# The causal mask of an attention stage moves from TensorE products into VectorE's row maximum

## The chip, the core and the metric

The kernel runs on one core of a Trainium2 chip. The metric is device time in microseconds: the median of three runs of the kernel before is 2123.16 us (2119.22 to 2128.04). The engines are called as in the profile: PE is TensorE, PEld its weight loads, DVE is VectorE, ACT ScalarE, POOL GpSimd, SP SyncE. All arithmetic is fp32, or fp32 split into a high and a low part for TensorE.

## The reference

Two blocks over x of 32 batches, 256 tokens, 256 features. Each block is a small conditional network, then a feed-forward part with experts. The change touches the attention in the first block:

```python
q = (x @ wq.T).reshape(B, S, N_HEADS, HEAD_DIM)        # 16 heads of 16
k = (x @ wk.T).reshape(B, S, N_KV_HEADS, HEAD_DIM)     # 4 key heads, each for 4 query heads
...
attn = jnp.einsum('bqhd,bkhd->bhqk', q, k) * scale
causal = jnp.tril(jnp.ones((S, S), dtype=bool))
attn = jnp.where(causal, attn, jnp.float32(-jnp.inf))
attn = jax.nn.softmax(attn, axis=-1)
out = jnp.einsum('bhqk,bkhd->bqhd', attn, v).reshape(B, S, C)
```

The stages around it are: a gated network whose weights are picked per batch (before it), the products of the eight routed experts, a second network with shared experts, and sixteen experts (after it).

## The kernel before

The kernel is written engine by engine, in program order, with semaphores between the engines; no scheduler reorders it. The attention stage runs over the 32 batches as a software pipeline. One call of `body(i)` on every engine works on several batches at once: the turned scores and exponentials of batch i, the scores and row maxima of batch i + 1, the projection of q, k and v of batch i + 2, the output projection of batch i - 2, and, for pairs of batches further back, the choice of experts (the picks, in every second call). An engine's order within a call is the order of the lines in its `body`.

Scores are made twice. First, with the queries on the partitions, to find each query's maximum over the keys (`scores`, L1708, and `maxima`, L1241). Then, with the keys on the partitions and the maximum subtracted inside the product (`turned_scores`, L1733), for the exponentials (`exps`, L1135), where GpSimd sets the later keys to zero (`keep_earlier`, L1035). The causal mask of the change is the one of the first scores only: it keeps later keys out of the maximum.

The first scores of a batch come in three rounds r. Rounds 0 and 1 take the second 128 queries (q = 1) with all 256 keys, two heads of each group a round. Round 2 takes the first 128 queries (q = 0) with the first 128 keys, all four heads. Each round fills four PSUM banks of 512 columns, one for each key head g, in a ring of six banks (`slot`, L886), which the turned scores use in turn with them. The products contract over 16 rows and four of them, at different rows of the array, run side by side. The mask is then added by one more product for each bank: a bf16 identity times a bf16 mask, on the 128 columns of each head in which later keys exist (L1729 to L1731). That product closes the bank and raises `scores_done`.

VectorE reduces each bank with one `tensor_reduce` to the negated maxima of its two or four heads (L1248) and raises `max_done`, twelve times a batch. TensorE waits for it at three kinds of places. It reuses a bank only when its maxima are taken (`ring_free`, L1704): the turned scores of round 0 (L1736) wait for the tenth maximum of the batch ahead, the scores of round 0 (L1712) for all twelve, those of round 1 and the turned scores of rounds 1 and 2 for others. And `turn_max` (L1773) transposes the maxima, for q = 0 when the twelfth is there, for q = 1 when the eighth is; the transposed row is copied (`keep_shift`, L1250 on VectorE and L1157 on ScalarE) and goes by a DMA into the row of the queries that the turned scores read.

In VectorE's `body` (L1516) the maxima stand between other work: `residual`, `keep_shift`, then maxima of round 0 with `norm_low` between the second and third, division and `h_low`, maxima of round 1 with `divide` and `keep_kv` between them, `keep_logits`, maxima (2, 0) and (2, 1), `out_low` (o_lo), maxima (2, 2) and (2, 3). In TensorE's `body` (L1850) the part around round 2 is: `turn_max(i, 1)`, `scores(i, 2)`, `turn_out`, `values(i, 0)`, and in the next call `turned_scores(i, 0)`, `project_out`, `turn_max(i, 0)`, `scores(i, 0)`.

The constants are prepared in the stage before: the load of `at.mask` (L196), its bf16 form and the bf16 identity on ScalarE (L308, L310).

Of the kernel before, what the change touches and what calls it, by code (L numbers as in the profile page):

```python
# [7 lines left out]
BF16 = mybir.dt.bfloat16  # L8
SP, PE = mybir.EngineType.SP, mybir.EngineType.PE
U32 = mybir.dt.uint32  # L10
ALU = mybir.AluOpType
# [3 lines left out]
P = 128  # L15
B, S, D = 32, 256, 256
TT = S // P
KT = D // P
# [53 lines left out]
class AttentionConstants:  # L72

    LOADS = 15
    HIGHS = 5 + 4 * KT
    LOWS = 2 + 4 * KT

    def __init__(self, nc, ctx, sem):
        def sb(name, shape, dt=F32):
            return ctx.enter_context(nc.sbuf_tensor(name, shape, dt))  # L80

        self.ident = sb("at_ident", [P, P])
        self.identb = sb("at_identb", [P, P], BF16)
        self.mask = sb("at_mask", [P, P])
        self.one_rows = sb("one_rows", [P, 1])
        self.maskb = sb("maskb", [P, G, P], BF16)
        self.norm = sb("at_norm", [P, KT])
        self.norm_q = sb("at_norm_q", [P, KT])
        self.wqk_raw = sb("wqk_raw", [P, KT, QB + 1, P])
        self.wqk_hi = sb("wqk_hi", [P, KT, QB + 1, P], F32R)  # L90
        self.wqk_lo = sb("wqk_lo", [P, KT, QB + 1, P], F32R)
        self.wv_raw = sb("wv_raw", [P, KT, VW])
        self.wv = sb("wv", [P, KT, 2 * VW], F32R)
        self.wo_raw = sb("wo_raw", [P, KT, D])
        self.wo_hi = sb("wo_hi", [P, KT, D], F32R)
        self.wo_lo = sb("wo_lo", [P, KT, D], F32R)
        self.norm2 = sb("norm2", [P, KT])
        self.gate_raw = sb("gate_raw", [P, KT, EM])
        self.gate = sb("gate", [P, KT, 2 * EM], F32R)
        self.earlier_raw = sb("earlier_raw", [P, P])  # L100
        self.earlier = sb("earlier", [P, P], BF16)
        self.ones = sb("ones", [P, P], BF16)
        self.iota = sb("expert_iota", [P, EM])
        self.region = sb("region", [P, EM])
        self.rules = sb("rules", [P, RULES])
        self.tile_index = sb("tile_index", [1, 3 * TILES0])
        self.own_row = sb("own_row", [P, EM])
        self.const_in = sem("at_const_in")
        self.w_hi_done = sem("at_w_hi_done")
        self.w_lo_done = sem("at_w_lo_done")  # L110


def cond_ffn_phase(nc, sem, x_t, w_ug, w_dn, cond, c0, at, front, norm_w, w_qk, one_rows, w_v, w_o, ident_in, mask_in, route_consts):
# [3 lines left out]
    with ExitStack() as ctx:  # L117
# [135 lines left out]
        def _(act):  # L253
# [50 lines left out]
            def weights_high(n):  # L304
                if n == 0:
                    act.wait_ge(at.const_in, 16 * at.LOADS)
                    nc.scalar.activation(at.norm_q[:], at.norm[:], ACT.Copy, scale=HD ** -0.5).then_inc(at.w_hi_done, 1)
                    nc.scalar.activation(at.identb[:], at.ident[:], ACT.Copy).then_inc(at.w_hi_done, 1)  # L308
                elif n == 1:
                    nc.scalar.activation(at.maskb[:], at.mask[:].unsqueeze(1).broadcast_to([P, G, P]), ACT.Copy).then_inc(at.w_hi_done, 1)  # L310
                    nc.scalar.activation(at.earlier[:], at.earlier_raw[:], ACT.Copy).then_inc(at.w_hi_done, 1)
                elif n in (2, 4):
                    t = n // 2 - 1
                    act.wait_ge(at.w_hi_done, 1)
                    nc.scalar.activation(at.wqk_hi[:, t, 0:QB], at.wqk_raw[:, t, 0:QB], ACT.Copy, scale=at.norm_q[:, t:t + 1]).then_inc(at.w_hi_done, 1)
                    nc.scalar.activation(at.wqk_hi[:, t, QB], at.wqk_raw[:, t, QB], ACT.Copy, scale=at.norm[:, t:t + 1]).then_inc(at.w_hi_done, 1)
                elif n in (3, 5):
                    t = n // 2 - 1
                    nc.scalar.activation(at.wv[:, t, 0:VW], at.wv_raw[:, t], ACT.Copy, scale=at.norm[:, t:t + 1]).then_inc(at.w_hi_done, 1)
                    nc.scalar.activation(at.gate[:, t, 0:EM], at.gate_raw[:, t], ACT.Copy, scale=at.norm2[:, t:t + 1]).then_inc(at.w_hi_done, 1)  # L320
                elif n == 6:
                    nc.scalar.activation(at.wo_hi[:], at.wo_raw[:], ACT.Copy).then_inc(at.w_hi_done, 1)
# [50 lines left out]
        def _(dve):  # L373
# [67 lines left out]
            def weights_low(n):  # L441
                if n == 1:
                    nc.vector.memset(at.ones[:], 1.0).then_inc(at.w_lo_done, 1)
                elif n in (2, 3, 4, 5):
                    t = n // 2 - 1
                    dve.wait_ge(at.w_hi_done, 2 * n + 2)
                    if n % 2 == 0:
                        parts = ((at.wqk_lo[:, t, 0:QB], at.wqk_raw[:, t, 0:QB], at.norm_q, at.wqk_hi[:, t, 0:QB]),
                                 (at.wqk_lo[:, t, QB], at.wqk_raw[:, t, QB], at.norm, at.wqk_hi[:, t, QB]))
                    else:  # L450
                        parts = ((at.wv[:, t, VW:2 * VW], at.wv_raw[:, t], at.norm, at.wv[:, t, 0:VW]),
                                 (at.gate[:, t, EM:2 * EM], at.gate_raw[:, t], at.norm2, at.gate[:, t, 0:EM]))
                    for lo, raw, norm, hi in parts:
                        nc.vector.scalar_tensor_tensor(out=lo, in0=raw, scalar=norm[:, t:t + 1], in1=hi.bitcast(F32),
                                                       op0=ALU.mult, op1=ALU.subtract).then_inc(at.w_lo_done, 1)
                elif n == 6:
                    dve.wait_ge(at.w_hi_done, at.HIGHS)
                    nc.vector.tensor_tensor(at.wo_lo[:], at.wo_raw[:], at.wo_hi[:].bitcast(F32), ALU.subtract).then_inc(at.w_lo_done, 1)
# [100 lines left out]

EPS = 1e-6  # L560
MASKED = -1e30
SLOTS = 6
EM = 8
REGION = B * S + P
# [154 lines left out]
def attention_phase(nc, sem, c0, at, front, x, sums, sorted_rows, results, routes, shared, we_source, later_weights, shared_sources, ended):  # L719

    with ExitStack() as ctx:
        def sb(name, shape, dt=F32):
            return ctx.enter_context(nc.sbuf_tensor(name, shape, dt))
# [13 lines left out]
        q_t = front.q_t + [sb(f"q_t{n}", [P, G, S]) for n in range(Front.BATCHES, 4)]  # L737
        k_t = front.k_t + [sb(f"k_t{n}", [P, S]) for n in range(Front.BATCHES, 4)]
        v = front.v + [sb(f"v{n}", [P, TT, NKV, 32]) for n in range(Front.BATCHES, 4)]
        neg_max = [sb(f"neg_max{q}", [P, NKV, G]) for q in range(2)]  # L740
        shift = [sb(f"shift{q}", [NH, P]) for q in range(2)]
        weights_diag1 = [sb(f"weights_diag1_{p}", [P, NKV, G * P]) for p in range(2)]
        weights_diag0 = sb("weights_diag0", [P, NKV, G * P])
# [381 lines left out]
        def _(act):  # L1125
# [30 lines left out]

            def keep_shift(i):  # L1157
                act.wait_ge(max_t_done, times(2, i, 3))
                nc.scalar.activation(shift[1][:], piece_b[0:NH, 0:P], ACT.Copy).then_inc(b_free, 1)

            def body(i):
                has, has_before, has_next = exists(i), exists(later(i, -1)), exists(later(i, 2))
# [77 lines left out]
        def _(dve):  # L1240
            def maxima(b, r, g):  # L1241
                dve.wait_ge(scores_done, times(12, b, 4 * r + g + 1))
                bank_ = slot(2 * r + 1, g)[:]
                if r < 2:
                    out, src = neg_max[1][:, g, 2 * r:2 * r + 2], bank_.rearrange("p (j s) -> p j s", j=2)
                else:
                    out, src = neg_max[0][:, g, :], bank_.rearrange("p (j s) -> p j s", j=G)
                nc.vector.tensor_reduce(out, src, AX_X, ALU.max, negate=True).then_inc(max_done, 1)  # L1248

            def keep_shift(i):  # L1250
                dve.wait_ge(max_t_done, times(2, i, 2))
                nc.vector.tensor_copy(shift[0][:], piece_b[0:NH, 0:P]).then_inc(b_free, 1)

            def by_head():
                return piece_a[:].rearrange("p (j g c) -> p j g c", j=G, g=NKV)
# [447 lines left out]
        def _(pe):  # L1703
# [4 lines left out]
            def scores(i, r):  # L1708
# [13 lines left out]
                for c, j in enumerate(heads_):  # L1722
                    for g in range(NKV):
                        rows = slice(32 * g, 32 * g + HD)
                        if r and c == 0 and g >= 2:
                            until(pe, exp_done, no_more_than(times(12, i, 4 * r + g - 1), 12 * B))
                        nc.tensor.matmul(slot(2 * r + 1, g)[:, c * keys:(c + 1) * keys], q_t[n][rows, j, q * P:(q + 1) * P], k_t[n][rows, 0:keys],  # L1727
                                         start=(c == 0), stop=False)
                for g in range(NKV):  # L1729
                    out = slot(2 * r + 1, g)[:].rearrange("p (c s) -> p c s", s=keys)[:, :, q * P:(q + 1) * P]  # L1730
                    nc.tensor.matmul(out, at.identb[:], at.maskb[:, 0:len(heads_), :], start=False, stop=True).then_inc(scores_done, 1)  # L1731

            def turned_scores(i, r):  # L1733

# [38 lines left out]
            def turn_max(i, q):  # L1773
                b = later(i, q)
                take_b(f"shift_q{q}", i)
                pe.wait_ge(max_done, times(12, b, 8 if q else 12))
                nc.tensor.transpose(piece_b[0:NH, 0:P], neg_max[q][:].rearrange("p g j -> p (g j)"), at.ident[:]).then_inc(max_t_done, 1)

            def heads(i, q):
                take_a(f"heads_q{q}", i)  # L1780
# [1413 lines left out]
def lay_out(inputs):  # L3194
# [13 lines left out]
    def by_slice(b):  # L3208
# [32 lines left out]
        "expert_gu": np.concatenate([by_rows(a[F1 + "Wg"]), by_rows(a[F1 + "Wu"])], 2),  # L3241
        "expert_d": by_rows(a[F1 + "Wd"]),
        "ident": eye,
        "causal": np.where(later, MASKED, 0.0).astype(np.float32),
        "expert_iota": to_all(np.arange(EM, dtype=np.float32)),
        "earlier": later.astype(np.float32),
        "region": to_all(REGION * np.arange(EM, dtype=np.float32)),
# [22 lines left out]
```

## Time and profile before

| | |
|---|---|
| median of three runs | 2123.16 us |
| span of the profiled execution | 2121.4 us |
| TensorE busy | 2043.6 us, 96% |
| VectorE busy | 1352.5 us, 64% |
| ScalarE busy | 1116.8 us, 53% |
| GpSimd busy | 966.6 us, 46% |
| row maxima (L1248) | 384, 683 ns each |
| mask products (L1731) | 384, median 282 ns |

The profile is one execution, taken by the hardware profiler. Busy time is the union of an engine's instructions. Instructions of one engine overlap in the records: one begins before the one in front of it has ended, so what an instruction costs its queue is the distance from its start to the start of the next, and not its duration. A merged row of the timeline gives the start, the time from the first start to the last end, and the count. Behind a row stands the idle time before it and what ended it.

### The profile page before, as it was taken

Reading aid. Unit: us, or ns where it says so; the run is one execution under the profiler, and the core shown is the slowest. Engines: PE = TensorE matmul, PEld = TensorE weight load, DVE = VectorE, ACT = ScalarE, POOL = GpSimd, SP = SyncE. Lnnn points to the kernel's source line nnn. Section 1 sums busy time; section 2 is a strip of 40 time slices with the busy share of each in tenths; the row PEclk is TensorE's granted clock in tenths of the full one; section 3 lists DMA queues with packets and bytes.
Section 4 is the critical chain, followed back from the end, with each engine's and each line's share of the span. In section 5 each row is a group of like instructions: output and inputs, shape, how many; then the busy total and the mean of one; then the engine's idle time right before and its main releaser. Section 6 shows DMA issues by size and latency. Waiting matters only on the chain. (4 is left out here: it accounts for less than half of the span.)

```text
span 2121.4 us, 47931 instructions
## 1 busy us (share of the span) xinstructions
PE 2043.6 (96%) x16392; PEld 1739.7 (82%) x16392; DVE 1352.5 (64%) x2818; ACT 1116.8 (53%) x2219; POOL 966.6 (46%) x1062
## 2 busy tenths in 40 slices
PE   7999989999999999989979999999899999999997
PEld 7999975666666666659978999999888888888886
DVE  7888955667667667774636777788645454545452
ACT  6777745666666666655543333344344444444442
POOL 0000003356556556546634444444255656565653
PEclk9999998999999999989989999999999999999999
DMA  7667711123233233228964444544245454545442
GB/s 289 265 262 264 264 51 42 57 97 100 87 104 108 88 103 94 69 89 291 310 216 147 147 149 151 171 144 153 88 106 113 95 114 94 114 93 115 91 87 30
DMA packets 134528, 289.21 MB, mean 136 GB/s; under 512 B 23009, under 2 KB 64738, under 8 KB 128098
## 3 DMA queue, kind: packets, MB, share of 16 engines
q1 hardware_dynamic: 84322, 176.99, 24.9%
q0 software_dynamic: 50048, 110.14, 20.2%
q8 instruction: 96, 1.57, 0.3%
q14 instruction: 62, 0.51, 0.1%
HBM read 186.90 MB, written 95.42 MB: 133 GB/s over the span
## 5 line engine op out<-in xcount | busy, mean ns | idle before, releaser
L1248 DVE TENSOR_REDUCE neg_max<-ring 128x2 f32<-128x512 f32 (+1 forms) x384 | 250.4, 683 | 89.9 <-PE ring L1731 88.0
L1041 POOL TENSOR_SCALAR_AFFINE_SELECT weights_diag<-weights_diag 128x512 f32<-128x512 f32 x256 | 157.5, 640 | 266.4 <-ACT weights_diag L1139 266.4
L2903 POOL DMA_INDIRECT out<-q_t,row_put x128 | 201.7, 1576 | 158.8 <-ACT q_t L2967 132.4
L3041 DVE TENSOR_TENSOR ex_hid<-ex_up_ps,gelu 128x512 f32<-128x512 f32 x128 | 86.9, 688 | 173.2 <-ACT gelu L2951 160.9
L2951 ACT ACTIVATE gelu<-ex_gate_ps 128x512 f32<-128x512 f32 x128 | 76.1, 596 | 188.5 <-PE ex_up_ps L62 183.7
L2374 POOL DMA_INDIRECT picked_rows<-results,lo_row_now x128 | 134.5, 1051 | 56.0 <-issue 29.6
L1139 ACT ACTIVATE weights_diag<-ring 128x512 f32<-128x512 f32 x256 | 138.5, 600 | 20.4 <-PE ring L1747 14.5
L60 PE MATMUL ex_down_ps<-ex_dn_lo,ex_hid_hi 128*128 128x256 f32 x512 | 144.4, 282 | 2.8 <-issue 2.8
L61 PE MATMUL ex_down_ps<-ex_dn_hi,ex_hid_lo 128*128 128x256 f32 x512 | 144.4, 282 | 0.0
L62 PE MATMUL ex_down_ps<-ex_dn_hi,ex_hid_hi 128*128 128x256 f32 x512 | 144.3, 282 | 0.0
L1049 POOL DMA_INDIRECT sorted_rows<-h_sb,row_now x128 | 126.6, 989 | 35.0 <-issue 35.0
L360 POOL DMA_DIRECT2D c<-c_sb x31 | 17.1, 552 | 273.3 <-DVE c_sb L430 273.3
L1727 PE MATMUL ring<-k_t,q_t 16*128 16x128 f32 (+1 forms) x2048 | 120.5, 348 | 10.2 <-DVE neg_max L1248 5.2
L1139 ACT ACTIVATE weights_full<-ring 128x512 f32<-128x512 f32 x128 | 66.1, 604 | 105.2 <-PE ring L1747 66.9
L1747 PE MATMUL ring<-q_t,k_t 17*128 17x512 f32 x768 | 111.5, 651 | 2.9 <-DVE neg_max L1248 2.5
L1727 PEld LDWEIGHTS ring<-k_t,q_t 16*128 16x128 f32 x2048 | 86.9, 189 | 31.9 <-issue 23.4
L3034 DVE TENSOR_TENSOR ex_xt_lo<-ex_turned,ex_xt_hi 128x512 fp32r<-128x512 f32 x64 | 41.2, 686 | 106.5 <-ACT ex_xt_hi L2945 98.6
L2958 ACT ACTIVATE ex_hid_hi<-ex_hid 128x512 fp32r<-128x512 f32 x128 | 79.1, 628 | 41.7 <-DVE ex_hid L3041 37.9
L2421 ACT ACTIVATE ht_hi<-turned 128x512 fp32r<-128x512 f32 x32 | 19.1, 598 | 154.6 <-PE turned L2708 154.6
L60 PEld LDWEIGHTS ex_down_ps<-ex_dn_lo,ex_hid_hi 128*128 128x128 f32 x512 | 96.2, 188 | 4.6 <-issue 3.3
L61 PEld LDWEIGHTS ex_down_ps<-ex_dn_hi,ex_hid_lo 128*128 128x128 f32 x512 | 96.4, 188 | 1.4
L62 PEld LDWEIGHTS ex_down_ps<-ex_dn_hi,ex_hid_hi 128*128 128x128 f32 x512 | 96.6, 189 | 0.0
(404 smaller groups left out, 7513.8 us busy)
## 6 DMA issues: line engine op xcount, KB each, us to landing
ug_raw<-in_w_ug SPq DMA_DIRECT2D x32, 1028.0 KB, 5.0
dn_raw<-in_w_dn SPq DMA_DIRECT2D x32, 640.0 KB
q_t<-sorted_rows SPq DMA_DIRECT2D x136, 128.0 KB
moe_w<-in_expert_gu SPq DMA_DIRECT2D x16, 1024.0 KB
results<-c0n POOLq DMA_DIRECT2D x33, 256.0 KB
x_raw<-in_x_t SPq DMA_DIRECT2D x32, 256.0 KB, 5.0
c0n<-c SPq DMA_DIRECT2D x32, 256.0 KB, 4.7
c0r<-c SPq DMA_DIRECT2D x32, 256.0 KB
```

Source lines behind the costliest of these rows:

```text
L60: nc.tensor.matmul(out, lhs_hi, rhs_lo, start=start, stop=False)
L61: nc.tensor.matmul(out, lhs_lo, rhs_hi, start=False, stop=False)
L62: return nc.tensor.matmul(out, lhs_hi, rhs_hi, start=False, stop=stop)
L1041: nc.gpsimd.affine_select(part, part, [[0, G], [1, P]], ALU.is_ge, 0.0, base=0, channel_multiplier=-1).then_inc(kept_done, 1)
L1049: nc.gpsimd.indirect_dma_start(out=sorted_rows, out_offset=to, in_=h_sb[b[1] % 4][:, t, :], in_offset=None).then_inc(scattered[b[1] % 2], 16)
L1139: nc.scalar.activation(tile[:, g, :], slot(2 * r, g)[:], ACT.Exp).then_inc(exp_done, 1)
L1248: nc.vector.tensor_reduce(out, src, AX_X, ALU.max, negate=True).then_inc(max_done, 1)
L1727: nc.tensor.matmul(slot(2 * r + 1, g)[:, c * keys:(c + 1) * keys], q_t[n][rows, j, q * P:(q + 1) * P], k_t[n][rows, 0:keys], start=(c == 0 ...
L1747: nc.tensor.matmul(slot(2 * r, g)[:], k_t[n][rows, k * P:(k + 1) * P], q_t[n][rows, :, q * P:(q + 1) * P], start=True, stop=True).then_inc ...
L2374: nc.gpsimd.indirect_dma_start(out=picked[par][:, n, :], out_offset=None, in_=results, in_offset=bass.IndirectOffsetOnAxis(ap=row_now[par] ...
L2903: nc.gpsimd.indirect_dma_start(out=out_rows, out_offset=bass.IndirectOffsetOnAxis(ap=at, axis=0), in_=eo[c][:, n, :], in_offset=None, comp ...
L3041: nc.vector.tensor_tensor(hid[f % 2][:], up_ps[f % 2][:], gelu[f % 2][:], ALU.mult).then_inc(hid_done, 1)
```

## The change

The mask products and their two bf16 constants go. The mask constant becomes 128 x 256, zeros beside the causal triangle, so that its whole width fits a head of 256 keys and its last 128 columns fit a head of 128. VectorE takes each head on its own: one `tensor_tensor_reduce` adds the mask to the head's scores, writes the sum back to PSUM and gives its maximum. That makes two of them in place of one `tensor_reduce` in rounds 0 and 1 and four in round 2. The maxima are no longer negated there; the two copies of the transposed row do that. TensorE's last score product of each bank closes it and raises `scores_done`.

```diff
-    HIGHS = 5 + 4 * KT
+    HIGHS = 3 + 4 * KT
...
-        self.identb = sb("at_identb", [P, P], BF16)
-        self.mask = sb("at_mask", [P, P])
+        self.mask = sb("at_mask", [P, S])
...
-        self.maskb = sb("maskb", [P, G, P], BF16)
...
-                    nc.scalar.activation(at.identb[:], at.ident[:], ACT.Copy).then_inc(at.w_hi_done, 1)
...
-                    nc.scalar.activation(at.maskb[:], at.mask[:].unsqueeze(1).broadcast_to([P, G, P]), ACT.Copy).then_inc(at.w_hi_done, 1)
...
+LOWEST = -3e38
...
-                nc.scalar.activation(shift[1][:], piece_b[0:NH, 0:P], ACT.Copy).then_inc(b_free, 1)
+                nc.scalar.activation(shift[1][:], piece_b[0:NH, 0:P], ACT.Copy, scale=-1.0).then_inc(b_free, 1)
...
                 if r < 2:
-                    out, src = neg_max[1][:, g, 2 * r:2 * r + 2], bank_.rearrange("p (j s) -> p j s", j=2)
+                    keys, first, out = S, 2 * r, row_max[1]
                 else:
-                    out, src = neg_max[0][:, g, :], bank_.rearrange("p (j s) -> p j s", j=G)
-                nc.vector.tensor_reduce(out, src, AX_X, ALU.max, negate=True).then_inc(max_done, 1)
+                    keys, first, out = P, 0, row_max[0]
+                for c in range(512 // keys):
+                    own = slice(c * keys, (c + 1) * keys)
+                    last = nc.vector.tensor_tensor_reduce(bank_[:, own], bank_[:, own], at.mask[:, S - keys:S], 1.0, LOWEST,
+                                                          ALU.add, ALU.max, out[:, g, first + c:first + c + 1])
+                last.then_inc(max_done, 1)
...
-                nc.vector.tensor_copy(shift[0][:], piece_b[0:NH, 0:P]).then_inc(b_free, 1)
+                nc.vector.tensor_scalar(shift[0][:], piece_b[0:NH, 0:P], -1.0, None, ALU.mult).then_inc(b_free, 1)
...
-                        nc.tensor.matmul(slot(2 * r + 1, g)[:, c * keys:(c + 1) * keys], q_t[n][rows, j, q * P:(q + 1) * P], k_t[n][rows, 0:keys],
-                                         start=(c == 0), stop=False)
-                for g in range(NKV):
-                    out = slot(2 * r + 1, g)[:].rearrange("p (c s) -> p c s", s=keys)[:, :, q * P:(q + 1) * P]
-                    nc.tensor.matmul(out, at.identb[:], at.maskb[:, 0:len(heads_), :], start=False, stop=True).then_inc(scores_done, 1)
+                        last = nc.tensor.matmul(slot(2 * r + 1, g)[:, c * keys:(c + 1) * keys], q_t[n][rows, j, q * P:(q + 1) * P], k_t[n][rows, 0:keys],
+                                         start=(c == 0), stop=(c == len(heads_) - 1))
+                        if c == len(heads_) - 1:
+                            last.then_inc(scores_done, 1)
...
-        "causal": np.where(later, MASKED, 0.0).astype(np.float32),
+        "causal": np.concatenate([np.zeros((P, P)), np.where(later, MASKED, 0.0)], 1).astype(np.float32),
```

## Rows read from the trace of the kernel before

**Rows 1.** The page: TensorE's busy time, and its granted clock in 40 slices.

```profile
PE 2043.6 (96%) x16392; PEld 1739.7 (82%) x16392; DVE 1352.5 (64%) x2818; ACT 1116.8 (53%) x2219; POOL 966.6 (46%) x1062
...
PEclk9999998999999999989989999999999999999999
```

**Rows 2.** Busy us by window (count), clock, DMA; then waits from 400 to 900.

```profile
400.47:900.10 499.63, 499.38 (x4923) 325.98 (x4923) 350.26 (x1000) 311.17 (x740) 279.45 (x360) 1.00 0.30 94
...
DVE neg_max L1248 <- PE ring L1731: 57.2, 49, 2.1
...
PEld ring L1747 <- DVE neg_max L1248: 21.0, 25, 0.8
```

**Rows 3.** Timeline of TensorE through one batch, and one row a batch later.

```profile
500.16 1.15 PE L1727 MATMUL ring<-k_t,q_t 16*128 16x256 f32 x16
501.23 0.33 PEld L1731 LDWEIGHTS ring<-maskb,at_identb 128*128 128x128 bf16 x4 [0.33 <-issue]
501.24 0.61 PE L1731 MATMUL ring<-maskb,at_identb 128*128 128x256 bf16 x4
...
501.68 0.60 PE L1788 MATMUL piece_b<-at_ident,normed 128*128 128x128 f32 x4
...
507.42 0.61 PE L1731 MATMUL ring<-maskb,at_identb 128*128 128x256 bf16 x4
...
507.87 0.60 PE L1782 MATMUL piece_a<-at_ident,ot_sb 128*128 128x128 f32 x4
...
513.68 1.17 PE L1727 MATMUL ring<-k_t,q_t 16*128 16x128 f32 x32
...
514.78 1.04 PE L1731 MATMUL ring<-maskb,at_identb 128*128 128x512 bf16 x4
...
515.66 0.60 PE L1788 MATMUL piece_b<-at_ident,o 128*128 128x128 f32 x4
...
517.18 1.14 PE L1747 MATMUL ring<-q_t,k_t 17*128 17x512 f32 x8
...
519.78 0.27 PE L1777 MATMUL piece_b<-at_ident,neg_max 128*16 128x128 f32 x1
...
539.79 0.27 PE L1777 MATMUL piece_b<-at_ident,neg_max 128*16 128x128 f32 x1
```

**Rows 4.** Timeline of VectorE in the same batch: maxima of round 0, then round 2.

```profile
501.56 1.29 DVE L1248 TENSOR_REDUCE neg_max<-ring 128x2 f32<-128x512 f32 x2 [0.32 <-PE ring L1731]
...
515.21 1.29 DVE L1248 TENSOR_REDUCE neg_max<-ring 128x4 f32<-128x512 f32 x2 [2.15 <-PE ring L1731]
...
516.92 0.69 DVE L1267 TENSOR_TENSOR o_lo<-piece_b,o_hi 128x512 fp32r<-128x512 f32 x1 [0.42 <-ACT o_hi L1155]
...
517.53 1.28 DVE L1248 TENSOR_REDUCE neg_max<-ring 128x4 f32<-128x512 f32 x2
```

**Rows 5.** VectorE's groups by form: count | busy us, mean ns | idle before.

```profile
L1248 DVE TENSOR_REDUCE neg_max<-ring 128x2 f32<-128x512 f32 x200 | 131.4, 683 | 7.6 <-PE ring L1731 5.8
...
L1264 DVE TENSOR_TENSOR o<-piece_a,rinv 128x256 f32<-128x256 f32 x50 | 20.9, 419 | 0.8
...
L685 DVE TENSOR_REDUCE v<-piece_b 128x64 f32<-128x128 f32 x50 | 12.0, 282 | 0.0
...
L1299 DVE MATCH_VALUE_LOAD top_at<-top,logits 128x8 f32 x52 | 3.2, 62 | 0.0
...
L1511 DVE TENSOR_TENSOR squares<-squares 128x128 f32<-128x128 f32 x14 | 4.1, 292 | 0.5
```

**Rows 6.** Timeline of ScalarE: a square with an accumulated sum, and its reading.

```profile
519.31 0.42 ACT L632 ACTIVATE squares<-c0n 128x256 f32<-128x256 f32 x1
...
519.62 0.20 ACT L632 ACTIVATION_READ_ACCUMULATOR squares<-c0n 128x1 f32 x1
```

**Rows 7.** Timeline of the last batches: VectorE's weights, TensorE waiting for a maximum.

```profile
917.37 1.41 DVE L1608 SCALAR_TENSOR_TENSOR moe_w<-moe_w,norm,we_hi 128x512 fp32r<-128x512 f32 x2
...
930.03 1.24 PE L1747 MATMUL ring<-q_t,k_t 17*128 17x512 f32 x4 [1.75 <-DVE neg_max L1248]
```

More of the change, by code:

```diff
@@ L445, in weights_low @@
                     t = n // 2 - 1
-                    dve.wait_ge(at.w_hi_done, 2 * n + 2)
+                    dve.wait_ge(at.w_hi_done, 2 * n)
                     if n % 2 == 0:
@@ L739, in attention_phase @@
         v = front.v + [sb(f"v{n}", [P, TT, NKV, 32]) for n in range(Front.BATCHES, 4)]
-        neg_max = [sb(f"neg_max{q}", [P, NKV, G]) for q in range(2)]
+        row_max = [sb(f"row_max{q}", [P, NKV, G]) for q in range(2)]
         shift = [sb(f"shift{q}", [NH, P]) for q in range(2)]
@@ L1776, in turn_max @@
                 pe.wait_ge(max_done, times(12, b, 8 if q else 12))
-                nc.tensor.transpose(piece_b[0:NH, 0:P], neg_max[q][:].rearrange("p g j -> p (g j)"), at.ident[:]).then_inc(max_t_done, 1)
+                nc.tensor.transpose(piece_b[0:NH, 0:P], row_max[q][:].rearrange("p g j -> p (g j)"), at.ident[:]).then_inc(max_t_done, 1)
             def heads(i, q):
```

## The prediction

> **What bounds the kernel now.** I read the page first, for engines and slices. TensorE is busy 96% of the span, at a granted clock of 9 tenths or more in all slices but three [rows 1]. The change touches the attention stage alone. In its steady part a table of windows shows TensorE busy in all but 0.25 us of 499.63 and VectorE in 350.26, that is 70% [rows 2]. The waits agree: VectorE's row maximum waits for the mask product 49 times, TensorE for the row maximum only in one place, the first turned scores of a batch, and there its weight load waits while its matmuls still run [rows 2]. So a batch costs what TensorE's queue costs: from the scores at 500.16 to the second following transpose of maxima at 539.79, plus the 0.20 until the scores behind it, is two batches in 39.83 us, 19.92 each [rows 3]. VectorE has about 6 us of slack in each, but not everywhere: between the last scores of a batch and the transpose of its maxima at 519.78 it has little, since the four heads' maxima of round 2 stand there with o_lo between them [rows 3, 4].
>
> **What is removed.** Twelve mask products a batch. On TensorE's queue, start of the group to start of the next instruction, they take 501.24 to 501.68, 507.42 to 507.87 and 514.78 to 515.66: 0.44 + 0.45 + 0.88 = 1.77 us [rows 3]. TensorE alone would need 19.92 - 1.77 = 18.15 us a batch. Times 32 batches that is 57 us, the ceiling of the gain. Two constants made by ScalarE in the first stage go too, and the mask's load becomes twice as large; both lie in the stage before, beside the products of the conditional network, and I cost them at nothing (a few tenths if that cover fails). Changing the sign in the two copies of the shift keeps their number and nearly their length: nothing.
>
> **What is added.** VectorE did 12 reductions of 512 elements a batch. Now it does 16 operations of 256 (rounds 0 and 1, two a group) and 16 of 128 (round 2, four a group), each of which adds a mask from SBUF, writes PSUM back and gives a maximum as a second output. No row shows this operation. Its price, start to start, is bounded so:
> - Two reductions of 683 ns fit in 1.29 us, so the second starts 0.60 after the first: 512 elements at 0.96 a ns are 0.533, and 0.07 is what an instruction adds [rows 4, 5]. An addition on 256 elements lasts 419 ns and a reduction of 128 lasts 282 ns, two of which fill 0.48: starts 0.20 apart [rows 5]. That is 0.20 for 128 elements and, by the same slope, 0.34 for 256.
> - The second output. ScalarE has the same form: its square with an accumulated sum shows as an ACTIVATE of 0.42 and a READ_ACCUMULATOR of 0.20 that starts 0.31 after it [rows 6]. I expect such a reading on VectorE. Its cheapest instruction, without a tensor output, lasts 62 ns [rows 5]. So low is no extra instruction at all (0.34 and 0.20), then +0.07 (0.41 and 0.27), high is one that overlaps with nothing and lasts as long as small VectorE operations do, 0.15: an addition on 128 elements is 292 ns [rows 5], so 0.44, and 0.57 for 256. I take 0.42 and 0.28: the pace of back-to-back rows plus the cheapest row, rounded up, as no operation here waits for the one before it.
>
> ScalarE's rows above show the reading. [...]
>
> **Who hides what.** I follow one batch from its first scores, at 0 (500.16), by rows 3 and 4.
> - Rounds 0 and 1. VectorE needs 8 x 2 x 0.42 = 6.7 us instead of 8 x 0.60 = 4.8. Each group is 0.24 longer. Round 0 can also begin a little earlier, as its release is now the last score product and not the mask product. The consumers are the scores of round 1 (the ring's slots), then the keys' product, then the transpose of round 1's maxima. Walking VectorE's queue with its other work (0.61 for low parts, 0.34 for divisions) I find it 0.3 to 0.5 us ahead of each consumer in a batch without the expert picks and about even in one with them. So these 1.9 us are hidden, narrowly; if an operation costs 0.05 more, 8 of them come out on the path.
> - Round 2. TensorE reaches these scores at 513.68 - 500.16 - 0.44 - 0.45 = 12.63. The first maximum started 1.53 behind them and will start about 1.1 behind them, since 0.43 of it was the mask product: 13.73. Two groups are 8 operations of b = 0.28, 2.24; with 0.15 for the end and the semaphore the turned scores start at 16.12. TensorE is there at 12.63 + 1.10 + (517.18 - 515.66) = 15.25: a stall of 0.9 us that was not there before. Then o_lo, 0.61, and two more groups, 2.24, and 0.15: at 18.97 the transpose of maxima may start its weights, and the next scores follow 0.30 later. TensorE, with 519.78 - 517.18 = 2.6 us of turned scores and projection behind 16.12, would be there at 18.7: another 0.2 to 0.3.
> So the period is 12.63 + 1.1 + 0.61 + 0.15 + 0.30 + 16 b = 14.79 + 16 b, and batches with picks have small operations and a prefix product in the same stretch, about 0.4 us: on average 15.0 + 16 b = 19.5 us. The gain is 0.42 us of the 1.77. Break-even is b = 0.31.
>
> **The sum.** Some 28 of the 32 batches run in that state: -0.42 x 28 = -12. The first ones fill the pipeline, in the slice from 318 to 371 us at a clock of 8 tenths [rows 1]; I give them nothing. In the last four VectorE also makes the low parts of the experts' weights, 1.41 us right behind the maxima of round 2, and once the tile lists; TensorE already waits 1.75 us for a maximum there [rows 7]. What I lengthen comes out in full: four times 0.8, +3. Together -9 us. The profiled execution spans 2121.4 us; the median of the runs, 2123.16, is 1.8 above it. 2123.2 - 9 = 2114.
>
> **Rivals.**
> - A: the one above, VectorE becomes the bound of round 2 and most of the gain is given back. b from 0.265 to 0.30, 2104 to 2122 us, 2114 in the middle. For it: back-to-back rows and the cheapest row. Chance 0.48.
> - B, slower: the same mechanism in the same place, but an operation costs more than 0.31 us for 128 elements, because the reading of the maximum does not overlap or the write to PSUM costs extra. At b = 0.33 and 0.47 for 256, 15.0 + 5.3 = 20.3 and 0.2 from rounds 0 and 1: +0.6 x 28 and some 6 at the end, 2146. At the high bound, 0.44 and 0.57, 22.0 + 0.8: +2.9 x 30, 2210. For it: three outputs or inputs that no row has together, 292 ns for an addition of 128, and that a schedule made by hand misses small stalls. Against it: the overlap that all rows show. Chance 0.40.
> - C: no reading instruction, b = 0.20, period 18.2, TensorE stays the bound: about 2070. Against it are the rows of ScalarE. Chance 0.07.
> - D: the change doesn't free what it removes. Before a mask product the weight loads wait 0.33 us for nothing that the profile shows, at the step from products on 16 rows to products on 128 [rows 3]; the next instruction behind the scores is on 128 rows too, and if the step costs it more than it did the mask, up to 0.4 a batch comes back and nothing is seen: 2119 to 2127. Chance 0.05.
>
> **The numbers.** The forecast is A's 2114. Half of A lies over 0.5% faster (below 2112.5), half within it; about 0.5% is what a measurement can tell here. Faster: 0.24 + 0.07 = 0.31; within: 0.24 + 0.05 = 0.29; slower: 0.40. I move 0.01 from each of the first two to the last for stalls that I missed: 0.30, 0.28, 0.42. The range leaves out C and the far part of B: 2100 to 2185.
>
> **What would show it.** Right: VectorE rows of about 0.29 us for 128 elements with a short reading after each, 0.28 a pair; VectorE busy 13.96 - 12 x 0.65 + 16 x 0.70 = 17.4 us of 19.5, 89%; TensorE about 93% busy in the stage, its waits at the turned scores of round 0 and the transpose of maxima, both for VectorE; scores and transposes elsewhere without waits; the stages after 958 unchanged in length. Wrong: waits at round 1's scores or the keys' product (rounds 0 and 1 were not hidden), a pair above 0.31 (B), no reading (C), or a clock below 1 in the steady stage.

## The result and the profile after

The changed kernel takes 2111.1 us (median of five runs, 2110.17 to 2115.33) where the kernel before takes 2123.96 (five runs, 2119.22 to 2128.04): the ratio is 0.994, with a 95% interval of 0.9921 to 0.9958. It is 0.6% faster, 12.9 us; 2114 was forecast. The profiled execution spans 2112.9 us against 2121.4.

The page of the changed kernel, as [rows 1]:

```profile
PE 2015.1 (95%) x16008; PEld 1716.8 (81%) x16008; DVE 1435.4 (68%) x4482; ACT 1115.9 (53%) x2217; POOL 963.3 (46%) x1062
...
PEclk9999986999999999989988999999899999999999
```

TensorE lost 384 products and 28.5 us of busy time, VectorE gained 1664 instructions and 82.9 us. The steady part of the attention stage, by window and by waits (as [rows 2]; behind the length stand the busy us and counts of PE, PEld, DVE, ACT and POOL, then the clock, the DMA share and GB/s):

```profile
400.00:880.00 480.00, 463.10 (x4576) 298.97 (x4579) 412.04 (x2292) 308.37 (x735) 278.02 (x359) 1.00 0.30 98
...
PEld ring L1747 <- DVE row_max L1247: 58.5, 50, 1.5
...
DVE ring L1247 <- PE ring L1728: 37.4, 25, 1.8
...
PE ring L1747 <- DVE row_max L1247: 14.7, 25, 0.6
```

TensorE, without a gap before, is idle for 16.9 of 480 us, 14.7 of them in 25 waits of 0.6 us in one place: the turned scores (L1747) wait for a row maximum. VectorE is busy 86% of the stretch. Its groups there, shapes kept apart, as [rows 5]:

```profile
L1247 DVE CUSTOM_DVE_ANT_0 ring<-ring,at_mask 128x256 f32<-128x256 f32 x400 | 157.7, 446 | 0.0
L1247 DVE DVE_READ_ACCUMULATOR2_ANT row_max<- 128x1 f32 x800 | 110.1, 138 | 0.0
L1247 DVE CUSTOM_DVE_ANT_0 ring<-ring,at_mask 128x128 f32<-128x128 f32 x400 | 101.9, 323 | 37.4 <-PE ring L1728 37.4
```

Each operation (CUSTOM_DVE_ANT_0, the fused addition and maximum) has a reading of its maximum behind it, of 138 ns. The timeline of VectorE in round 2, as [rows 4], tells what the pair costs:

```profile
515.46 0.30 DVE L1247 CUSTOM_DVE_ANT_0 ring<-ring,at_mask 128x128 f32<-128x128 f32 x1 [1.80 <-PE ring L1728]
515.68 0.14 DVE L1247 DVE_READ_ACCUMULATOR2_ANT row_max<- 128x1 f32 x1
515.68 0.33 DVE L1247 CUSTOM_DVE_ANT_0 ring<-ring,at_mask 128x128 f32<-128x128 f32 x1
515.93 0.14 DVE L1247 DVE_READ_ACCUMULATOR2_ANT row_max<- 128x1 f32 x1
515.93 0.33 DVE L1247 CUSTOM_DVE_ANT_0 ring<-ring,at_mask 128x128 f32<-128x128 f32 x1
...
517.42 0.69 DVE L1268 TENSOR_TENSOR o_lo<-piece_b,o_hi 128x512 fp32r<-128x512 f32 x1
518.02 0.29 DVE L1247 CUSTOM_DVE_ANT_0 ring<-ring,at_mask 128x128 f32<-128x128 f32 x1
```

The next operation starts at the same time as the reading (515.68), and behind the first operation, which takes 0.22, the starts are 0.248 us apart: eight operations fill 515.46 to 517.42. For 256 elements they are 0.382 apart:

```profile
299.60 0.47 DVE L1247 CUSTOM_DVE_ANT_0 ring<-ring,at_mask 128x256 f32<-128x256 f32 x1
299.98 0.14 DVE L1247 DVE_READ_ACCUMULATOR2_ANT row_max<- 128x1 f32 x1
299.98 0.46 DVE L1247 CUSTOM_DVE_ANT_0 ring<-ring,at_mask 128x256 f32<-128x256 f32 x1
```

TensorE through one batch, as [rows 3]:

```profile
501.36 1.15 PE L1728 MATMUL ring<-k_t,q_t 16*128 16x256 f32 x16
...
502.61 0.66 PE L1788 MATMUL piece_b<-at_ident,normed 128*128 128x128 f32 x4
...
507.15 1.32 PE L1728 MATMUL ring<-k_t,q_t 16*128 16x256 f32 x16
508.40 0.65 PE L1782 MATMUL piece_a<-at_ident,ot_sb 128*128 128x128 f32 x4
...
514.27 1.17 PE L1728 MATMUL ring<-k_t,q_t 16*128 16x128 f32 x32
515.38 0.66 PE L1788 MATMUL piece_b<-at_ident,o 128*128 128x128 f32 x4
...
517.62 1.14 PE L1747 MATMUL ring<-q_t,k_t 17*128 17x512 f32 x8 [0.59 <-DVE row_max L1247]
...
520.26 0.27 PE L1777 MATMUL piece_b<-at_ident,row_max 128*16 128x128 f32 x1
520.49 0.71 PE L1728 MATMUL ring<-k_t,q_t 16*128 16x256 f32 x8
```

From the scores of round 0 to those of round 2 it takes 12.91 us (13.52 before, by [rows 3]), from there to the transpose of maxima (L1777) 5.99 (6.10 before). The first part gained, the second hardly did.

### The profile page after: what moved, and what is told of

It is laid out like the page before. It is cut to its first block and busy times, and to the rows that moved or that the text cites. A ratio compares the mean times of both kernels' runs of the same rounds, so it can differ in the third digit from the quotient of the medians.

```text
span 2112.9 us, 48825 instructions
## 1 busy us (share of the span) xinstructions
PE 2015.1 (95%) x16008; PEld 1716.8 (81%) x16008; DVE 1435.4 (68%) x4482; ACT 1115.9 (53%) x2217; POOL 963.3 (46%) x1062
## 5 line engine op out<-in xcount | busy, mean ns | idle before, releaser
L1247 DVE CUSTOM_DVE_ANT_0 ring<-ring,at_mask 128x128 f32<-128x128 f32 (+1 forms) x1024 | 332.0, 385 | 64.7 <-PE ring L1728 64.7
L1247 DVE DVE_READ_ACCUMULATOR2_ANT row_max<- 128x1 f32 x1024 | 141.0, 138 | 0.0
L1747 PE MATMUL ring<-q_t,k_t 17*128 17x512 f32 x768 | 114.8, 668 | 22.9 <-DVE row_max L1247 22.4
L1747 PEld LDWEIGHTS ring<-q_t,k_t 17*128 17x128 f32 x768 | 31.3, 190 | 85.6 <-DVE row_max L1247 80.0
```

The lines of the kernel that those rows point to most:

```text
L1247: last = nc.vector.tensor_tensor_reduce(bank_[:, own], bank_[:, own], at.mask[:, S - keys:S], 1.0, LOWEST, ALU.add, ALU.max, out[:, g, fir ...
L1747: nc.tensor.matmul(slot(2 * r, g)[:], k_t[n][rows, k * P:(k + 1) * P], q_t[n][rows, :, q * P:(q + 1) * P], start=True, stop=True).then_inc ...
```

## The experiments

For every kernel the trace gives 64 transposes of the maxima, two a batch. The steady batch is the distance from the 9th to the 57th, over 24. For the kernel before that is (871.98 - 393.98) / 24 = 19.92, for the changed one (860.50 - 398.50) / 24 = 19.25, from these rows:

```profile
398.50 0.27 PE L1777 MATMUL piece_b<-at_ident,row_max 128*16 128x128 f32 x1
...
860.50 0.27 PE L1777 MATMUL piece_b<-at_ident,row_max 128*16 128x128 f32 x1
```

All kernels in that way, in us ("start" is the start of the 11th transpose, "end" the distance from the 55th to the 64th, "rest" the span minus the 64th):

| kernel | median | ratio to before (95%) | span | batch | start | end | rest |
|---|---|---|---|---|---|---|---|
| before | 2123.96 | 1 | 2121.4 | 19.92 | 414.0 | 92.0 | 1177.3 |
| before_again | 2123.5 (one run) | | 2121.8 | 19.91 | 418.6 | 91.8 | 1173.3 |
| after | 2111.1 | 0.9921 to 0.9958 | 2112.9 | 19.25 | 417.7 | 94.8 | 1176.9 |
| after_again | 2110.6 | 0.9915 to 0.9957 | 2109.2 | 19.25 | 418.7 | 90.5 | 1176.4 |
| e1_vector_part | 2150.3 | 1.0089 to 1.0163 | 2145.0 | 20.41 | 420.6 | 97.4 | 1177.9 |
| e2_no_mask | 2082.9 | 0.9762 to 0.9822 | 2081.8 | 18.32 | 413.4 | 86.3 | 1179.2 |
| e3_products_round2 | 2110.7 | 0.9898 to 0.9952 | 2106.2 | 19.15 | 417.0 | 91.0 | 1176.9 |
| e4_products_rounds01 | 2134.4 | 1.0022 to 1.0049 | 2138.6 | 19.99 | 423.8 | 93.7 | 1181.3 |
| e5_weights_earlier | 2107.2 | 0.9894 to 0.9938 | 2107.0 | 19.25 | 419.2 | 88.5 | 1175.9 |
| e6_norm_later | 2107.4 | 0.9900 to 0.9941 | 2107.7 | 19.26 | 414.1 | 94.0 | 1176.0 |
| e8_round2_both | 2101.3 | 0.9874 to 0.9921 | 2097.7 | 19.14 | 412.7 | 91.0 | 1172.9 |
| e9_before_both | 2122.5 | 0.9978 to 1.0008 | 2123.2 | 19.92 | 416.9 | 91.1 | 1177.1 |
| e10_extra_round2 | 2120.8 (one run) | | 2119.2 | 19.56 | 420.2 | 92.8 | 1175.8 |
| e11_extra_round0 | 2113.8 (one run) | | 2112.1 | 19.27 | 418.8 | 94.3 | 1175.2 |

**Each engine's part alone.** First VectorE's, with the products kept: the kernel before gets the change's lines in `maxima` and in the two copies of the shift, and `scores` stays as it was:

```diff
-                nc.vector.tensor_reduce(out, src, AX_X, ALU.max, negate=True).then_inc(max_done, 1)
+                for c in range(512 // keys):
+                    own = slice(c * keys, (c + 1) * keys)
+                    last = nc.vector.tensor_tensor_reduce(bank_[:, own], bank_[:, own], at.mask[:, S - keys:S], 1.0, LOWEST,
+                                                          ALU.add, ALU.max, out[:, g, first + c:first + c + 1])
```

> VectorE's part of the change alone, on the kernel before: the 32 operations a batch that add the mask and take the maximum stand in VectorE's queue, while the twelve mask products stay on TensorE (the mask is added twice). Theory (round 2 is bound by VectorE, its period is 15.0 + 16 b with b the start-to-start time of a 128-element operation, 0.248 in the trace of after): the products of round 2, 0.88 us, delay the first maximum by what they last, so some 0.4 to 0.9 us come on top: a batch takes 20.2 to 20.5 us instead of 19.92, the kernel 8 to 20 us longer than before (2132 to 2144). Rival (VectorE's new work is hidden everywhere and only TensorE's queue counts): a batch takes 19.9 and the kernel the time of before, within 5 us.

A batch takes 20.41 us, +0.49, and the kernel 23 us more than the runs of before beside it (2126.9): VectorE's work is not hidden. The batch lies in the expected range and the time 6 us beyond the expected 2132 to 2144: 22 steady batches make 11 of the 23 us, and the start and the end of the stage lost 4 to 7 and 5 us more (420.6 against 414.0 and 418.6, 97.4 against 92.0 and 91.8). Then TensorE's:

```diff
-                for g in range(NKV):
-                    out = slot(2 * r + 1, g)[:].rearrange("p (c s) -> p c s", s=keys)[:, :, q * P:(q + 1) * P]
-                    nc.tensor.matmul(out, at.identb[:], at.maskb[:, 0:len(heads_), :], start=False, stop=True).then_inc(scores_done, 1)
```

> TensorE's part alone, on the kernel before: the mask products are gone and VectorE keeps its twelve reductions of 512 elements a batch; the causal mask of the row maximum is left out (the maximum is taken over later keys too). Theory: TensorE's queue is the bound, a batch takes 19.92 - 1.77 = 18.15 us, and the kernel 28 to 32 x 1.77 = 50 to 57 us less than before (2067 to 2074): what after doesn't reach is VectorE's doing. Rival (part of the products' time is not given back, since the step from products on 16 rows to products on 128 costs the next instruction what it cost the mask product): a batch takes 18.5 us or more, the kernel gains under 45 us.

A batch takes 18.32, a gain of 1.60 of the 1.77, and the kernel 44 us less, not 50 to 57. TensorE's trace shows where the missing 0.17 stays. The transposes that follow each of the three rounds of scores take 0.05 to 0.06 more, start to start, than they did behind a mask product: 0.58 here (511.58 to 512.16),

```profile
510.50 1.15 PE L1727 MATMUL ring<-k_t,q_t 16*128 16x256 f32 x16
...
511.58 0.66 PE L1787 MATMUL piece_b<-at_ident,normed 128*128 128x128 f32 x4
...
512.16 1.06 PE L1767 MATMUL piece_a<-weights_diag,v 128*32 128x512 f32 x8
```

and 0.53 in the kernel before (501.68, by [rows 3], to this row):

```profile
502.21 1.06 PE L1768 MATMUL piece_a<-weights_diag,v 128*32 128x512 f32 x8
```

The transposes last 0.66, and in [rows 3], behind the mask products, 0.60; three such places make 0.16. That is rival D's place, the step from products on 16 rows to products on 128, at under half its size: it allowed 0.4 a batch. What in the step costs the time is not shown. Both theories of this run were right in part. The difference from e2 to after, 19.25 - 18.32 = 0.93 us a batch, is what VectorE's part takes back.

At 2082.9 us e2 is the fastest kernel of the study. A maximum that counts the later keys too is never below the one that is wanted, the division by the sum cancels what is subtracted too much, and the later keys' weights are set to zero behind the exponential in any case (`keep_earlier`). So in exact arithmetic the result is the same; what the mask in the maximum guards is the range, as a much larger score of a later key could drive all the kept exponentials to zero. No run here tries such an input.

**Which round binds.** The change was split by rounds. The diff is e3's, against the changed kernel; e4 has `r < 2` in both places where e3 has `r == 2`:

```diff
+                if r == 2:
...
+                    nc.vector.tensor_reduce(out, src, AX_X, ALU.max).then_inc(max_done, 1)
+                    return
...
+                        masks = r == 2
...
+                for g in range(NKV if masks else 0):
+                    out = slot(2 * r + 1, g)[:].rearrange("p (c s) -> p c s", s=keys)[:, :, q * P:(q + 1) * P]
+                    nc.tensor.matmul(out, at.identb[:], at.maskb[:, 0:len(heads_), :], start=False, stop=True).then_inc(scores_done, 1)
```

> The change in rounds 0 and 1 only: in round 2 the four mask products and the single reduction of 512 elements a group stay as before. Theory (round 2 is what binds the new kernel, by its 16 operations on VectorE): TensorE's queue binds again, a batch takes 19.92 - 0.89 = 19.03 us, against 19.23 in the trace of after; the kernel comes out 3 to 8 us below the time of after (2103 to 2108), and the waits for row maxima at the turned scores of round 0 are gone. Rival (the 16 operations of rounds 0 and 1 bind): no better than after, 2111 to 2120.

> The change in round 2 only: rounds 0 and 1 keep their eight mask products and their single reduction of 512 elements a group. Theory (round 2 binds): the 0.89 us of products come back on TensorE in front of a stretch that VectorE sets: 15.0 + 0.89 + 16 x 0.248 = 19.86 us a batch, the kernel 2117 to 2124, as before. Rival (rounds 0 and 1 bind the new kernel): 19.1 us a batch or less, the kernel at or below the time of after (2111).

The four kernels make a square. Rounds 0 and 1 changed: 19.92 to 19.15 with the old round 2, 19.99 to 19.25 with the new one, that is -0.77 and -0.74. Round 2 changed: 19.92 to 19.99 and 19.15 to 19.25, +0.07 and +0.10. The two add up. All of the steady gain comes from rounds 0 and 1, and round 2 as changed is a small loss: its products were worth 0.83 (e3 to e2), its sixteen operations cost 0.93 (e2 to after). Both figures count the operations of rounds 0 and 1 as free, and the square bears that out: those two rounds gave 0.77, where their products were worth 0.44 + 0.45 less the 0.11 that e2 shows to stay. The waits for row maxima in e3, over the same 480 us:

```profile
PEld ring L1759 <- DVE row_max L1247: 21.0, 25, 0.8
...
PEld ring L1759 <- DVE row_max L1255: 14.3, 17, 0.8
```

Only weight loads wait, at most 0.8 us, under matmuls that run; the 0.6 us in which the matmuls themselves stood still are gone. The total of e3 missed the expected 2103 to 2108, as its median equals that of after; its steady part, 19.15 for 19.03, is right to 0.12 us a batch, and what varies beside it is told below. Of e4 the batch of 19.99 is 0.13 above the expected, and the kernel is 0.36% slower than before: 2134.4 us for the expected 2117 to 2124. Its profile is of the longest of its ten runs, 17 us longer than the first of before: the steady part explains 1.6 us of that (22 batches of +0.07), its late start, 423.8, some 10, and its end and rest 2 and 4.

**VectorE's bound measured directly.** One operation is added to VectorE's `body`, in e10 as the diff has it, in e11 behind `maxima(s, 0, 0)`:

```diff
                 if has_scores:
                     maxima(s, 2, 0)
+                    nc.vector.tensor_tensor(spare[:], at.mask[:], at.mask[:], ALU.add)
                     maxima(s, 2, 1)
```

> The changed kernel with one operation more on VectorE in each batch, an addition of two 128x256 tiles of SBUF into a spare tile (some 0.34 us start to start), between the first two maxima of round 2. Theory (VectorE sets the end of round 2): it comes out whole, the steady batch is 19.25 + 0.34 = 19.6 us, the kernel 10 to 12 us longer than the changed one. Rival (TensorE is the bound there and VectorE only close behind): under 0.15 a batch.

> The changed kernel with the same additional operation between the first two maxima of round 0. Theory (rounds 0 and 1 have slack on VectorE, 0.3 to 0.5 us before each consumer): a steady batch within 0.1 us of 19.25, the kernel within 4 us of the changed one. Rival (rounds 0 and 1 bind too, and the walk of VectorE's queue in the prediction had too much slack): 0.25 us a batch or more.

It costs 0.34 us of the queue, as these rows of e10 show, from its start to the next one's:

```profile
500.62 0.42 DVE L1591 TENSOR_TENSOR spare<-at_mask 128x256 f32<-128x256 f32 x1
500.96 0.29 DVE L1248 CUSTOM_DVE_ANT_0 ring<-ring,at_mask 128x128 f32<-128x128 f32 x1
```

In round 2 a batch grows by 0.31 us (19.25 to 19.56), in round 0 by 0.02. TensorE's waits over 400 to 880 us follow, e10 first, then e11:

```profile
PE ring L1749 <- DVE row_max L1248: 22.1, 25, 0.9
```

```profile
PE ring L1749 <- DVE row_max L1248: 14.6, 25, 0.6
```

So the bound is shown: in round 2 VectorE's queue sets the steady batch, and a delay in round 0 is absorbed before it gets there. Round 1 had no operation added of its own; that it is free too rests on the square above.

**The start and the end of the stage.** Both kernels were profiled a second time, and two edits made to the changed one. In e5 (first diff) the low parts of the experts' weights are made one body later, ahead of round 2's maxima and not behind them; in e6 (second) the low part of the normed rows goes behind the maxima of round 0, in the first body alone:

```diff
+                low_weights(later(i, -1))
                 if has_scores:
                     maxima(s, 2, 0)
...
-                for part in weight_parts(i):
...
```

```diff
-                if has_next:
+                if has_next and not is_at(i, START):
                     front.norm_low(dve, i[1] + 2)
                 if has_scores:
                     maxima(s, 0, 2)
                     maxima(s, 0, 3)
+                if is_at(i, START):
+                    front.norm_low(dve, i[1] + 2)
```

> The kernel before, unchanged, profiled a second time, to see how much of the difference at the start of the attention stage is the kernel's. Theory (the start of the stage is the same each time): the eleventh transpose of maxima again near 414 us, 100.5 after the first, with the granted clock back at 1.00 in 310 to 320. Rival (it varies from execution to execution): 2 us or more away from that.

> The changed kernel, unchanged, profiled and timed a second time beside its two edits below. Theory (the start and the end of the stage lose the same each time): from the first to the eleventh transpose of maxima again about 104 us, and the batch behind the last row maxima again about 24 us long instead of 20; the time 2108 to 2114. Rival (these losses vary from execution to execution): 2 us or more away.

> The changed kernel, with VectorE's making of the low parts of the experts' weights moved from behind the last maxima of a body to ahead of the first maximum of round 2, one body later. Theory (the last batches lose time because TensorE's transposes wait for the copy of the shift, which stands behind these two operations of 1.2 us, and then run at the lower clock): the batch of 24 us is 20 again, the kernel 3 to 5 us below the changed one. Rival (the loss comes from elsewhere, or the operations cost the same in the new place, where VectorE is the bound as well): within 1.5 us of the changed kernel.

> The changed kernel, with VectorE's low part of the normed rows moved behind the last two maxima of round 0, in the first body alone. In the traces of both kernels TensorE's second scores wait 4.6 to 6.2 us at 300 us for these maxima, which stand behind the low part, which waits for ScalarE, which waits for a DMA of the rows. Theory (that order costs the start of the stage, and TensorE's idle time there brings the lower clock): the wait is under 1.5 us, the stage starts 2 to 3 us earlier, and with the clock back earlier the kernel is 3 to 8 us below the changed one. Rival (the DMA sets the start anyway and TensorE idles a little later instead): within 1.5 us of the changed kernel.

The start is not the same each time: the eleventh transpose of the kernel before starts at 414.0 in one profile and at 418.6 in the other. The windows from 320 to 350 us differ in the clock, 0.77 in the first and 0.60 in the second; that of after is below (columns as above):

```profile
320.00:350.00 30.00, 27.74 (x157) 15.96 (x160) 14.99 (x81) 12.52 (x30) 7.94 (x13) 0.50 0.13 42
```

There TensorE's clock is at its 1.2 GHz level, behind an idle time of 6.07 us at 300 us (4.61 and 5.38 in the profiles of before); in both profiles of after it is 0.50 through that window. The end of the stage varies too, 94.8 and 90.5 in the two profiles of the changed kernel, and 92.0 and 91.8 before. In the first profile of the changed kernel a batch near the end took 24.1 us, in the second 21.5, and in those of before 20.1. These rows of VectorE and TensorE, from the first, show why:

```profile
886.35 2.23 DVE L1609 SCALAR_TENSOR_TENSOR moe_w<-moe_w,norm,we_hi 128x512 fp32r<-128x512 f32 x2
...
889.37 0.27 DVE L1253 TENSOR_SCALAR shift<-piece_b 16x128 f32<-16x128 f32 x1
```

```profile
889.69 1.11 PE L1788 MATMUL piece_b<-at_ident,normed 128*128 128x128 f32 x4 [2.29 <-DVE shift L1253]
```

The weights' low parts stand between the last maximum and the copy of the transposed row, and TensorE's transposes wait 2.29 us for that copy; they then last 1.11 instead of 0.66, at a granted clock of 0.50. The second profile has the same wait and keeps the full clock, 1.00:

```profile
890.77 0.66 PE L1788 MATMUL piece_b<-at_ident,normed 128*128 128x128 f32 x4 [2.29 <-DVE shift L1253]
```

So the wait belongs to the change and costs some 2 us each time; the 2.6 us more of the first profile go with its lower clock. In e5 the wait is gone at this place (that batch is 19.34), the end is 88.5, and the median is 3.4 us below that of after_again, within the expected 3 to 5, with ranges that don't touch (2104.01 to 2108.59, 2109.95 to 2110.99). In e6 the second scores start 2.7 and 2.9 us earlier than in the two profiles of after; the wait before them is still above the 1.5 expected, as the row shows:

```profile
303.12 2.09 PE L1730 MATMUL ring<-k_t,q_t 16*128 16x256 f32 x16 [2.77 <-DVE row_max L1247]
```

Its median is 3.2 us below after_again (2106.96 to 2109.29).

**All that helped together, and a control.**

> Three edits together: the change in rounds 0 and 1 only (products and single reductions stay in round 2), the weights' low parts one body later, and in the first body the rows' low part behind the maxima of round 0. Theory (each acts in a place of its own): a batch of 19.15 us instead of 19.25, worth 3 us; 3 us for the start; little for the weights, since with the single reductions the batch behind the last maxima was 19.5 us already: 2103 to 2106, ratio to before 0.990 to 0.9915. Rival (the steady gain of round 2 is lost again at the ends, or the two moves collide with the single reductions): 2107 or more.

> The kernel before with the two moves alone (the weights' low parts one body later; in the first body the rows' low part behind the maxima of round 0), as a control of whether their gain belongs to the change. Theory (the wait at the start is 4.6 to 5.4 us there too, the loss at the end isn't there: its batch is 20.1 us): 2 to 4 us below the kernel before, from the start alone. Rival (TensorE's queue hides both): within 1 us of it, and a steady period above 19.92 if the moved operations are in the way there.

e8 is e3 with the edits of e5 and e6; e9 is the kernel before with those two. e8 is the fastest of the kernels that keep the mask in the maximum, 2101.3 us, 1.0% below before (interval 0.8% to 1.3%) and 9 to 10 us below the changed kernel; 2103 to 2106 was expected. e9 gains nothing that can be measured, where I had expected 2 to 4 us: its first transpose is 2.5 us earlier than in before (310.97 against 313.46), but the eleventh, at 416.9, lies between the two profiles of before. Why the earlier start lasts in e6 and e8 and not in e9 is open; a trace of one execution each, with a clock that returns at different times, can't tell.

## Why the prediction was right, and where it was not

**The mechanism: right.** Rival A was forecast: VectorE becomes the bound of round 2, with a stall at the turned scores of round 0. It stands there, 0.59 us for 0.9 forecast, and e10, e11 and the square of four kernels show that round 2 is the one place. "Rounds 0 and 1 hidden, narrowly" was right and too cautious: a further 0.34 us in round 0 costs 0.02. The transposes of maxima wait little (5.99 us instead of 6.10 after the scores of round 2), and VectorE is 86% busy for 89% forecast, TensorE 96% for 93%.

**The price of an operation: too high.** I took b = 0.28 for 128 elements and 0.42 for 256; the rows give 0.248 and 0.382, between the bound without a reading (0.20, 0.34) and mine. The 0.248 lies below all of A's own range of b, 0.265 to 0.30. ScalarE's row was the right hint that a reading exists. What I got wrong was its cost: 138 ns long, it takes some 0.05 us of the queue by that bound, where I had put 0.08, as the next operation starts with it. The rule that an accumulator output makes two instructions (the Trainium skill, "VectorE: DVE Perf Modes", section "Two Vector instructions with no wait between them") is confirmed for VectorE by the 800 readings behind 800 operations; that page of the Trainium skill states it for Vector instructions alone, and for ScalarE it is [rows 6] that show it. The section "The DRAIN you can't avoid" of the same page (the Trainium skill, "VectorE: DVE Perf Modes") says that the next operation waits for an empty pipe, but also that "A next op that is not held starts earlier". The trace agrees with that exception: an operation of 0.33 us is followed by the next one's start after 0.25.

**The constant: too low.** 15.0 + 16 x 0.248 is 18.97, and the batch takes 19.25. The 0.28 missing are these, from the rows of TensorE and VectorE above. From the scores of round 0 to those of round 2 I had 12.63 and it is 12.91: twice the 0.05 to 0.06 that e2 shows behind a round without its mask product, and 0.17 more behind the scores of round 0, where in every second batch the transposes now wait for the copy of the transposed row (501.36 to 502.61 is 1.25; it is 1.08 in the batches between and in e2). Round 2 adds 0.09, as its first maximum starts 1.19 behind the scores and not 1.1. That makes this batch 19.13 (501.36 to 520.49); the mean is 0.12 more, as the batches between are longer (520.49 to 539.82 is 19.33), and for them I had allowed 0.2: 0.28 + 0.09 - 0.09. I named the first mechanism as rival D and didn't put its smaller form into the sum. The two errors have opposite signs, -0.51 and +0.28, so the gain is 0.67 a batch instead of 0.42.

**The sum.** Steady: 22 batches from the 11th to the 55th transpose, 438.2 us before and 423.5 after, -14.6. Start: 0 was forecast for the first batches; means of two profiles each, 416.3 and 418.2, +1.9. The forecast's 28 batches are all but the last four, so this "nothing" was not carried into its sum; in the trace 22 are steady. End: +3 was forecast and it is +0.8 in the same way (91.9 and 92.7, where the two profiles of after alone are 4.3 apart). At the steady gain these 4.5 batches would have given 3.0, so 3.8 were lost there, by the mechanism named: the wait behind the weights' low parts. Together -11.9 at the end of the stage, and -12.9 in the medians. So the steady term was too small, the loss at the end was rightly placed and too large as a net term, and the start, where the same kernel differs by 4.6 us, can't be told to better than that.

**Luck.** That 2114 lies 3 us from the result is in part luck. With the measured b alone my sum would have been 2123.2 - 0.95 x 28 + 3 = 2100, the very edge of the range; with the constant right too, 2123.2 - 0.67 x 28 + 3 = 2107. The price, the constant and the number of batches were off, in ways that in part cancel.

**Rivals.** C needed a batch of 18.2, which no operation of this price gives; B's point was b = 0.31, and 0.248 is well short of it. B had 0.40, which was too much for a price whose nearest rows were 0.20 and 0.27. By its own sum A's lower bound, b = 0.265, gives 2107 and not 2104. The 12.9 us are just over the half per cent that I had called "faster"; the forecast, 2114, lay just under it.

## What to carry to other kernels

Removing work from the bound engine pays only until the next engine binds, and that is read stage by stage: here VectorE was busy 70% of the steady part on average and had slack in two rounds out of three. Split such a change by place before keeping it whole: the part in which one operation of 0.60 us became four of 0.25 cost more than the products that it saved. Put the price of a new operation on a start-to-start basis, from rows where nothing waits, and try the moved bound by adding one small operation at each place.

## What the runs showed of the hardware

An operation with a second, accumulated output shows as two records on VectorE, and the reading overlaps with the next operation: 0.248 us apart for 128 elements and 0.382 for 256, with a tensor read from and written to PSUM in place and a second one read from SBUF. An addition of 256 elements in SBUF without such an output took 0.34, 0.04 less. Four transposes on TensorE that follow products on 16 rows last 0.66 us, and behind a product on 128 rows 0.60. At the start of the stage TensorE idles for 4.6 to 6.1 us, after which its clock, 0.50 of full speed, returned at different times in two executions of the same kernel: their first transposes were 0.4 us apart and their eleventh 4.6. And one and the same wait of 2.29 us near the end was followed by the full clock in one execution and by 0.50 in another; the batch took 21.5 and 24.1 us.
